# Four layers of graph message passing: the sorted rows are turned back in two rounded halves, and another engine writes them into the ring

## The reference

```python
# layer 0: relu([h[dst], h[src], edge_attr] @ W1 + b1) @ W2 + b2, summed by dst
# layer 1: softmax of e over the edges of each dst; sum of a * h[src]; elu
# layer 2: segment_max((h[dst] - h[src]) @ theta.T + theta_b + phi(h)[src])
# layer 3: an MLP of three products on [h[src], h[dst], edge_feat], mean by dst
h = jnp.maximum(_layernorm(x, axis=-1), 0.0)
x = x + _L1_gnn_ref(h, edge_weight1, src, dst)
h = jnp.maximum(_layernorm(x, axis=-1), 0.0)
x = x + _L2_gnn_ref(h, L2_gnn_theta_w, ..., src, dst)
```

## Time and profile before

| | |
|---|---|
| median of 3 runs | 7393.57 us |
| the runs | 7389.63 to 7395.25 us |
| profiled execution, its own time | 7395.24 us |
| its span in the profile | 7392.8 us |
| busy: TensorE / its weight loads | 6278.6 / 4961.4 us |
| busy: VectorE, ScalarE, GpSimd | 5448.2, 3494.3, 5400.2 us |
| mean granted clock of TensorE | 0.904 of 2.4 GHz |

### The profile page before, as it was taken

How to read it: one execution, slowest core, us unless ns; L and a number is a source line. 1 busy time by engine, 2 the same in 40 slices (tenths; PEclk the granted TensorE clock), 3 DMA queues, 4 the chain that set the end, 5 groups by cost and what they waited for, 6 DMA issues and landing times.

```text
span 7392.8 us, 107737 instructions
## 1 busy us (share of the span) xinstructions
PE 6278.6 (85%) x33032; PEld 4961.4 (67%) x33032; DVE 5448.2 (74%) x7602; ACT 3494.3 (47%) x7219; POOL 5400.2 (73%) x5687
## 2 busy tenths in 40 slices
PE   0799999999769888888479999999129999999995
PEld 0577777777557777777468888888116777677774
DVE  6888888888778777777666667777557777777773
ACT  5144444444336666666544445555115555555552
POOL 7777777777767777777766666777777777777776
PEclk9999999999868888888678999999569999999996
DMA  9366666666535555555334444555225555555552
GB/s 338 85 168 160 157 156 155 156 155 155 143 80 125 118 120 121 118 124 119 81 81 115 116 119 126 137 137 132 50 64 141 143 143 143 143 144 142 144 141 82
DMA packets 1085919, 975.11 MB, mean 132 GB/s; under 512 B 583086, under 2 KB 831400, under 8 KB 1085256
## 3 DMA queue, kind: packets, MB, share of 16 engines
q1 hardware_dynamic: 885508, 765.05, 36.6%
q0 software_dynamic: 183184, 160.61, 13.9%
q10 hardware_dynamic: 16692, 42.58, 1.5%
HBM read 601.42 MB, written 366.23 MB: 131 GB/s over the span
## 4 chain that ended last, share of the span: by engine, by line
PE 29%; POOL 28%; issue 10%; DVE 3%; DMA 2%; ACT 1%; SPq 0%; POOLq 0%; DVEq 0%; ACTq 0%
POOL G L847 23%; PE pScope L1219 9%; PE pEven L1245 6%; PE pScope L1133 4%; POOL R L868 2%; PE pEven L1335 2%; DMA G<-table,idx 2%; PE pScope L1210 1%; POOL R_hidden L868 1%; PE pT L1321 1%; POOL first_rows L808 1%; PE pScope L1354 1%; PE pScope L1342 1%; PE pEven L1342 1%; PE pEven L1285 1%
## 5 line engine op out<-in xcount | busy, mean ns | idle before, releaser
L847 POOL DMA_INDIRECT G<-table,idx x2770 | 2614.8, 944 | 849.7 <-issue 816.0
L847 POOL DMA_INDIRECT G<-table,e_dst x2218 | 2093.7, 944 | 849.1 <-issue 652.6
L1661 DVE TENSOR_TENSOR_SCAN K<-mask_f,K,pT 48x512 f32<-48x512 bf16 x782 | 1005.5, 1286 | 764.6 <-PE pT L1321 616.6
L1219 PE MATMUL pScope<-h_high,slot_onehot 128*128 (+1 forms) x2964 | 1264.8, 427 | 0.0
L977 ACT ACTIVATE K<-pT 48x512 f32<-48x512 f32 x782 | 461.6, 590 | 1550.1 <-PE pT L1321 1537.1
L1219 PE MATMUL pScope<-h_low,slot_onehot 128*128 (+1 forms) x2964 | 1168.7, 394 | 0.0
L1245 PE MATMUL pEven<-sorted_rows,turn_onehot 128*128 128x48 f32 x7296 | 1009.8, 304 | 87.4 <-ACT turn_onehot L1035 86.5
L1245 PEld LDWEIGHTS pEven<-sorted_rows,turn_onehot 128*128 128x128 f32 x7296 | 982.8, 220 | 94.0 <-ACT turn_onehot L1035 92.9
L1764 DVE TENSOR_REDUCE sorted_rows<-pScope 128x96 f32<-128x960 f32 x456 | 504.7, 1148 | 452.6 <-PE pScope L1233 447.0
L1321 PE MATMUL pT<-ident,G 128*112 128x128 f32 x3128 | 482.8, 277 | 408.5 <-DMA G<-table,idx 405.3
L1354 PEld LDWEIGHTS pScope<-ident,S 128*128 128x128 f32 x3128 | 498.1, 203 | 373.7 <-issue 360.7
(11 more groups left out here) (270 smaller groups left out, 10863.8 us busy)
## 6 DMA issues: line engine op xcount, KB each, us to landing
prefix<-O_hidden SPq DMA_DIRECT2D x390, 512.0 KB
mask_f<-same_row SPq DMA_DIRECT2D x392, 256.0 KB
prefix<-O SPq DMA_DIRECT2D x194, 512.0 KB
mask_f<-slot_rows SPq DMA_DIRECT2D x228, 416.0 KB
G<-first_rows SPq DMA_DIRECT2D x784, 96.0 KB
mask_f<-place_rows SPq DMA_DIRECT2D x228, 256.0 KB
G<-table,idx POOLq DMA_INDIRECT x2770
first_rows<-zeros ACTq DMA_DIRECT2D x14, 2688.0 KB, 16.6
```

The lines of the kernel that those rows point to most:

```text
L847: pool.indirect_dma_start(rows[:, slot, j, 0:widths[l]], None, table[l], bass.IndirectOffsetOnAxis(ap=at[:, n, j:j + 1], axis=0))\
L1219: pe.matmul(out, slot_onehot[:, k % 2, slot, :], part[:, bass.ds(row, SPAN_BYTES)].bitcast(f32r), start=False, stop=False)
L1661: dve.tensor_tensor_scan(K[r, c.slot, :], mask_of(c, r), pT[c.slot % 2][r, :], K[r, (c.slot - 1) % RING, CHUNK - 1:CHUNK], ALU.mult, ALU.add)\
```

## The change

The rows that a scope yields are split into a high half, rounded to float32r, and a low half, what the rounding left, and both are turned at once:

- ScalarE's `round_rows` writes `rows_high`, the rounded copy of `sorted_rows` (192 elements). It waits for the reductions and for the turn of the scope before, and stands right ahead of `mark_turn`.
- VectorE's `keep_low` subtracts it from `sorted_rows` into `rows_low` (192 elements, both operands in SBUF). It waits for the rounding.
- TensorE still makes 16 products a scope; each has 96 columns (high and low side by side) and float32r operands. It waits for `rows_halved` in place of `rows_reduced`.
- The placing moves from ScalarE to VectorE: a reduction by addition over the pair of halves (384 elements in, 192 out) into the ring, at other steps (`PLACE_AT`).
- `sorted_rows` has one buffer instead of two, so a reduction waits for the subtraction of the scope before.
- Two semaphores are merged into others (`idx4_in`, `iota_set`).

```diff
-    PLACE_AT = {l: [max(then - 3, CH * SCOPES[scope][0] - 6) for scope, then in zip(LAYER_SCOPES[l], at[1:] + [at[-1] + 3])]
+    PLACE_AT = {l: [max(then - 4, CH * SCOPES[scope][0] - 5) for scope, then in zip(LAYER_SCOPES[l], at[1:] + [at[-1] + 3])]
...
-        turn_onehot = over("slot_onehot end", "S", "turn_onehot", [P, SCOPE, SCOPE, P], f32)
-        place_onehot = over("turn_onehot end", "S", "place_onehot", [P, SCOPE, P], bf16)
+        turn_onehot = over("slot_onehot end", "S", "turn_onehot", [P, SCOPE, SCOPE, P], f32r)
+        rows_split = over("turn_onehot end", "S", "rows_split", [P, SCOPE, 2, D], f32r)
+        rows_high, rows_low = (rows_split[:, :, i, :] for i in range(2))
...
-        sorted_rows = over("slot_row end", "K", "sorted_rows", [P, 2, SCOPE, D], f32)
+        sorted_rows = over("slot_row end", "K", "sorted_rows", [P, SCOPE, D], f32)
...
-                def place_scope(k, l=l):
-
-                    act.wait_ge(scope_turned, SCOPES_BEFORE[l] + k + 1)
-                    half, j = SCOPES[LAYER_SCOPES[l][k]]
-                    slot, n = half * CH % RING, min(CH, NCH - half * CH)
-                    if half >= 2:
-                        act.wait_ge(rows_taken[l], CH // 2 * (half - 1))
-                    act.activation(G4[:, slot:slot + n, j, 0:D], turned[:, 0:n * D].rearrange("p (u d) -> p u d", d=D), ACT.Copy)\
-                       .then_inc(scope_placed, 1)
+                def round_rows(k, l=l):
+
+                    act.wait_ge(rows_reduced, 2 * (SCOPES_BEFORE[l] + k + 1))
+                    if SCOPES_BEFORE[l] + k:
+                        act.wait_ge(scope_turned, SCOPES_BEFORE[l] + k)
+                    act.activation(rows_high, sorted_rows[:, :, :], ACT.Copy).then_inc(rows_rounded, 1)
...
-                    pe.wait_ge(rows_reduced, 2 * (SCOPES_BEFORE[l] + k + 1))
+                    pe.wait_ge(rows_halved, SCOPES_BEFORE[l] + k + 1)
...
-                        last = pe.matmul(turned[:, u * D:(u + 1) * D], turn_onehot[:, t, u, :], sorted_rows[:, k % 2, t, :],
+                        last = pe.matmul(turned[:, u, :, :], turn_onehot[:, t, u, :], rows_split[:, t, :, :],
...
-                    if k >= 2:
-                        dve.wait_ge(scope_turned, SCOPES_BEFORE[l] + k - 1)
+                    if SCOPES_BEFORE[l] + k:
+                        dve.wait_ge(rows_halved, SCOPES_BEFORE[l] + k)
...
+                def keep_low(k, l=l):
+
+                    dve.wait_ge(rows_rounded, SCOPES_BEFORE[l] + k + 1)
+                    dve.tensor_tensor(rows_low, sorted_rows[:, :, :], rows_high.bitcast(f32), ALU.subtract)\
+                       .then_inc(rows_halved, 1)
+
+                def place_scope(k, l=l):
+
+                    dve.wait_ge(scope_turned, SCOPES_BEFORE[l] + k + 1)
+                    half, j = SCOPES[LAYER_SCOPES[l][k]]
+                    slot, n = half * CH % RING, min(CH, NCH - half * CH)
+                    if half >= 2:
+                        dve.wait_ge(rows_taken[l], CH // 2 * (half - 1))
+                    dve.tensor_reduce(G4[:, slot:slot + n, j, 0:D], turned[:, 0:n, :, :].rearrange("p u i d -> p u d i"),
+                                      AX, ALU.add).then_inc(scope_placed, 1)
...
                         for k in scopes_at(l, step, REDUCE):
                             reduce_rows(k)
+                        for k in [k for k, at in enumerate(PLACE_AT[l]) if at == step]:
+                            place_scope(k)
+                        for k in scopes_at(l, step, TURN[0]):
+                            keep_low(k)
```

More of the change, by code:

```diff
@@ L311, in build @@
         slot_onehot = over("K", "S", "slot_onehot", [P, 2, SLOTS, P], f32r)
-        turn_onehot = over("slot_onehot end", "S", "turn_onehot", [P, SCOPE, SCOPE, P], f32)
-        place_onehot = over("turn_onehot end", "S", "place_onehot", [P, SCOPE, P], bf16)
+        turn_onehot = over("slot_onehot end", "S", "turn_onehot", [P, SCOPE, SCOPE, P], f32r)
+        rows_split = over("turn_onehot end", "S", "rows_split", [P, SCOPE, 2, D], f32r)
+        rows_high, rows_low = (rows_split[:, :, i, :] for i in range(2))
+        place_onehot = over("rows_split end", "S", "place_onehot", [P, SCOPE, P], bf16)
         slot_values = over("place_onehot end", "S", "slot_values", [P, SCOPE, SLOTS], bf16)
@@ L370, in build @@
         scope_sum = pScope[:, :, :].rearrange("p t c -> p (t c)")
-        turned = pH1[0][:, 0:SCOPE * D]
+        turned = pH1[0][:, 0:SCOPE * 2 * D].rearrange("p (u i d) -> p u i d", i=2, d=D)
         work = pH2[0]
@@ L495, in build @@
         scope_placed = sem("scope_placed")
+        rows_rounded = sem("rows_rounded")
+        rows_halved = sem("rows_halved")
         turned_out = per_layer("turned_out", STREAMED)
@@ L617, in _ @@
                 if l == 0:
-                    sp.dma_start(idx4, src4_in).then_inc(idx4_in, 16)
+                    sp.dma_start(idx4, src4_in).then_inc(idx_in, 16)
                 rows_view = prefix[l].rearrange("(n p j) d -> n p (j d)", p=P, j=TJ)
@@ L794, in _ @@
                       channel_multiplier=PICK_GROUPS).then_inc(node_id_set, 1)
[L795 to L796 removed]
+            pool.iota(iota_i[:, 0:P], pattern=[[1, P]], base=0, channel_multiplier=0).then_inc(node_id_set, 1)
+            pool.iota(iota_i[:, P:P + 1], pattern=[[1, 1]], base=1, channel_multiplier=1).then_inc(node_id_set, 1)
             pool.memset(ident[:, :], 0.0).then_inc(ident_set, 1)
@@ L828, in _ @@
                 if l == 1:
-                    pool.wait_ge(idx4_in, 16)
+                    pool.wait_ge(idx_in, 32)
                     pool.wait_ge(G4_zeroed, 1)
@@ L1063, in _ @@
                     for step in range(-SLOTS_LOAD, 2 * DUOS):
-                        for k in [k for k, at in enumerate(PLACE_AT[l]) if at == step]:
-                            place_scope(k)
                         for k in scopes_at(l, step, TURN[0]):
+                            round_rows(k)
                             mark_turn(k, range(0, 2))
@@ L1544, in _ @@
             link(dve.memset(carry_scan[:, 0:1], -BIG))
-            dve.wait_ge(iota_set, 2)
+            dve.wait_ge(node_id_set, 5)
             for i in range(2):
```

4 lines of the change are left out of this document (1 added, 3 removed).

## The result

| | before | after |
|---|---|---|
| median | 7393.82 us | 7267.55 us (4 runs, 7263.24 to 7267.87) |
| ratio, 95% interval | | 0.9829, 0.9812 to 0.9846 |
| profiled execution, its span | 7395.24, 7392.8 us | 7267.87, 7266.0 us |
| layer 1, start of its first gather to that of its last | 1463.6 us | 1465.2 us |
| layer 2, the same | 1439.0 us | 1312.5 us |

A forecast was written before the change was run, and what follows sets the result against it. GpSimd issuing gathers was taken to bound layer 1; in layer 2, GpSimd's waits for late transposes left at most 137 us to gain. 7395 - 137 + 9 + 10 + 6 + 1 = 7284 us, range 7256 to 7380.

The forecast's parts named there:

- Layer 1 bound by GpSimd, layer 2 by TensorE with 137 us to win: Layer 1: GpSimd issues gathers without slack; layer 2: GpSimd waits for late transposes, at most 137 us to gain.
- The sum: Whole kernel: 7395 - 137 + 9 + 10 + 6 + 1 = 7284 us, with layer 1 adding 0.
- The bound's 137: Layer 2: its gathers fall from 1440 us to GpSimd's own 1303, saving 137 us.
- the 9 at the start: Start of layer 2: 9 us stay while the ring fills and TensorE sums its first scopes slowly.
- The 10 for unsteadiness: Layer 2: an allowance of 10 us left for unsteadiness.
- The 6 for gathers held up: GpSimd, 228 scopes: the subtraction's two SBUF reads delay gathers, 6 us in all, at most 57.
- The product: TensorE's turn: each new 96-column product takes 0.115 us, so a turn takes 1.84 us instead of 3.59.
- the stall of the earlier trace: Layer 2: ScalarE's copy waits 7.75 us for VectorE's transpose, delaying the marks, once in four scopes; it was to go.
- The clock falls more often: Rival, chance 0.12: idle TensorE loses clock in one of three layer 2 scopes, about 5 us each; 7339 us.
- The subtraction always meets a gather: Rival, chance 0.07: a fixed rhythm makes every subtraction delay a gather, 57 us in place of 6; 7335 us.
- Layer 1 loses: Rival, chance 0.15: VectorE's addition waits 4.8 us a scope for the slow turn in layer 1, 235 us more; 7519 us.
- its threshold of 2.4 us: Layer 1: VectorE's wait for the turn slows the layer only from 2.4 us a scope on.

The follow-up runs named there:

- the table alone: Kernel before with one figure of PLACE_AT changed, CH * half - 5 in place of - 6, moving 16 copies of layer 2 one step later: 7298.70 us.
- ScalarE placing: Changed kernel with the placing back on ScalarE, which copies only the high half; the low half is still rounded, subtracted and turned: 7277.68 us.
- the high half alone: Changed kernel without the low half: no subtraction, 16 products of 48 columns, VectorE copies instead of adding: 7276.73 us.
- 137 scopes: Changed kernel with 137 scopes in layer 2 instead of 130, nothing left out: 7250.55 us.
- 110 scopes in layer 1: Changed kernel with 147 scopes in layer 2 and 110 instead of 98 in layer 1: 7291.78 us.

## Why the prediction was right, and where it wasn't

- **Layer 1 bound by GpSimd, layer 2 by TensorE with 137 us to win:** right. 1045 gathers take 1312.5 us against a bound of 1303. That TensorE bounds once the stall is gone, and only there, is what the table alone (1340.9, TensorE 760 of 761 us) and the turn made twice (1343.1) show.
- **The sum.** Forecast -111, measured -127. The bound's 137 and the 9 at the start stand: 1303 + 9 = 1312. The 10 for unsteadiness were 0. The 6 for gathers held up were 3.4 over both layers (1.5 in layer 2, 1.9 in layer 1). The model was right, a gather that begins in a subtraction waits for it. Its size wasn't: at most 0.18 us for the 0.25 taken, and a loss for one subtraction in six.
- **The product** at 0.115 us, taken from transposes with such weight loads: 0.113 (1.81 / 16). That the load sets it is likely, as said above.
- **"the stall of the earlier trace rows loses its cause: the addition stands on the engine that transposes, in order behind it"**: the step that the runs don't bear out. The wait was seen rightly, and a placing on VectorE can't hold up ScalarE's marks. But the stall doesn't need the other engine to go: it was 16 copies that the table put ahead of the marks, and one step later on ScalarE they cost nothing (98 us back, 1340.9 for 1439.0). The prediction never asked why one scope in four was different, and its costing passed over the line of the diff that answers it. The forecast of layer 2 held all the same, since with the shorter turn TensorE makes up for such waits wherever they come from (ScalarE placing, 1315.1 us).
- **What stays open.** On VectorE the old figure couldn't have stood: a placing at step 4 x half - 6 would come ahead of the very transpose that it waits for. So the engine was never moved without the table. On ScalarE it could have stood; a halved turn with the old table there wasn't tried.
- **How the gain divides.** By the order in which the parts were taken away, 98 us come from those 16 steps, some 30 from the halved turn. Without the shorter turn the layer stops at 1341 us. With it, ScalarE's late copies may come back (the copy of the high half) and it still reaches 1315. So the parts aren't a plain sum: the room that the turn makes swallows such waits too.
- **The clock falls more often:** it did, but less often than the rival had it, and for less. TensorE waits for the reductions 60 times in 130 scopes. The lower clock shows in 31 sums, one in four and not one in three; it was 16 before. Such a sum takes 8.4 us in the mean for 6.6, 1.8 more (2.5 in the one shown) and not 5: 1.8 x 31 / 130 = 0.4 us a scope, which fits in what TensorE has to spare.
- **The subtraction always meets a gather:** it does (128 of 130 in layer 2), but mostly one that had begun before it, and such a gather loses nothing. The rhythm doesn't fix the place: 59 gathers of 2218 begin inside a subtraction. The Trainium skill, "SBUF — State Buffer", section "Who interferes with whom", infers that descriptor generation is spared. The 1.12 us for 0.94 speak against that for these indirect DMAs, as the earlier trace rows did.
- **Layer 1 loses:** its threshold of 2.4 us isn't contradicted by the runs, its wait was wrong. It charged the slow turn to all 98 scopes; with a turn as long as the one before, the mean wait was 2.2.

## What to carry to other kernels

When a stall comes in a fixed rhythm, count its occurrences and look for the same number in the tables that set the order; a single figure may be the cause, and the cheapest experiment is to change it alone. When a mean shows almost nothing, split the cases by which of the two engines began first: here it hid a wait that comes in one of the two orders alone. An engine that is exactly at its bound passes on such late waits as these, while one with 15% to spare swallows the same waits, so a shortened stage and a removed stall overlap and must not be summed. After such a change, the balance between engines is to be set anew: here 17 scopes more turned from a loss of 2.6%, of which the waits of ScalarE's copies may have their part, into a gain of 0.5%.

## What the runs showed of the hardware

- A turn's record takes 0.117 to 0.118 us at a clock of 0.99 for 48 columns in float32 and for 96 in float32r, and halving the columns at float32r changes it by 2%: behind a weight load of 128 columns, 96 moved columns cost hardly more than 48 here.
- An indirect DMA's issue on GpSimd that begins while VectorE runs a subtraction with both operands in SBUF (192 elements, 0.35 us) is held up, by up to 0.18 us (1.12 for 0.94). One that began before the subtraction isn't (0.944 in the mean, 169 cases). Over all subtractions this makes 0.013 to 0.015 us each.
- In five of the runs (ScalarE placing, the high half alone, 137 scopes, 110 scopes in layer 1, and the kernel before with 147 scopes) the 2770 gathers of the untouched layers took 0.946 us in the mean in place of 0.944, 6 to 7 us in all, and those of layers 1 and 2 were longer too. Kernels of both kinds are among them, so no edit here sets it; what does is open.
